# A layer norm's apply step divided between GpSimd and VectorE

## The reference, cut to what matters

```python
def _layernorm(x, axis=-1, eps=1e-05):
    m = jnp.mean(x, axis=axis, keepdims=True)
    v = jnp.var(x, axis=axis, keepdims=True)
    return (x - m) / jnp.sqrt(v + eps)
...
x = x + mixer(_layernorm(x))          # four times,
x = x + feed_forward(_layernorm(x))   # in turn
```

## Time and profile before

| | us |
|---|---|
| median of 3 runs | 810.92 (805.61 to 813.16) |
| the profiled execution: time | 812.87 |
| its span, first to last instruction | 811.2 |
| TensorE busy in the span | 668.7 (82%) |
| VectorE busy | 387.0 (48%) |
| ScalarE busy | 303.1 (37%) |
| GpSimd busy | 229.2 (28%) |

### The profile page before, as it was taken

The page is one execution under the profiler, slowest core; times in us unless marked ns, Lnnn a source line. Parts: engine busy times, 40 slices in busy tenths (PEclk is TensorE's granted clock), DMA queues, the critical chain, the costliest instruction groups (busy, mean ns, idle before and its releaser), DMA issues. The chain is left out here.

```text
span 811.2 us, 12856 instructions
## 1 busy us (share of the span) xinstructions
PE 668.7 (82%) x4034; PEld 556.4 (69%) x4034; DVE 387.0 (48%) x978; ACT 303.1 (37%) x604; POOL 229.2 (28%) x274
## 2 busy tenths in 40 slices
PE   4888936997996999957989983799995798898397
PEld 2476725685794899953677763699994367776296
DVE  4566816114445433314578756343440466885301
ACT  2344524232413344422434552235442243454222
POOL 5176620001200044442045400724334204541000
PEclk9989977798996899985899995899998589999599
DMA  3745720634206166533497503577653349840442
GB/s 90 195 114 142 176 57 0 156 99 96 48 1 175 40 161 160 121 48 65 131 248 212 111 17 113 149 177 183 170 124 48 70 132 233 222 114 1 102 119 72
DMA packets 92485, 95.14 MB, mean 117 GB/s; under 512 B 17313, under 2 KB 78644, under 8 KB 92424
## 3 DMA queue, kind: packets, MB, share of 16 engines
q1 hardware_dynamic: 78952, 74.91, 34.6%
q0 software_dynamic: 11808, 18.38, 11.3%
q10 hardware_dynamic: 1680, 1.28, 0.6%
HBM read 66.92 MB, written 27.84 MB: 117 GB/s over the span
## 5 line engine op out<-in xcount | busy, mean ns | idle before, releaser
L2017 POOL DMA_INDIRECT sum_scratch<-area,f_row_index x48 | 72.4, 1509 | 177.6 <-DVE area L1963 167.9
L881 DVE TENSOR_REDUCE neg_max<-psum 128x4 f32<-128x1024 f32 x72 | 87.9, 1221 | 31.0 <-PE psum L767 30.2
L1722 PE MATMUL psum<-w,area 128*112 128x192 f32 (+1 forms) x576 | 96.2, 326 | 0.0
L1722 PEld LDWEIGHTS psum<-w,area 128*112 128x112 f32 (+1 forms) x576 | 93.5, 183 | 0.0
L961 POOL TENSOR_TENSOR shift<-ident,neg_max 128x256 fp32r<-128x256 f32 x96 | 66.5, 704 | 84.8 <-DVE neg_max L881 56.4
L779 PE MATMUL psum<-q_parts,k_parts 128*128 128x256 f32 x288 | 78.5, 303 | 0.4
L780 PE MATMUL psum<-shift,ones_r 128*128 128x256 f32 x288 | 74.2, 289 | 0.0
L767 PE MATMUL psum<-k_parts,q_parts 128*128 128x256 f32 x288 | 52.9, 307 | 19.9 <-DVE neg_max L881 8.6
L1821 DVE TENSOR_TENSOR q_parts<-w,q_parts 128x1536 fp32r<-128x1536 f32 x16 | 28.1, 1758 | 82.7 <-ACT q_parts L1751 82.7
L779 PEld LDWEIGHTS psum<-q_parts,k_parts 128*128 128x128 f32 x288 | 56.7, 197 | 10.8 <-issue 8.2
L360 PE MATMUL psum<-ident,x_norm 128*96 128x128 f32 x128 | 26.1, 349 | 45.0 <-DVE x_norm L330 44.8
(11 more groups left out here) (250 smaller groups left out, 1328.9 us busy)
## 6 DMA issues: line engine op xcount, KB each, us to landing
w<-in_f_w_dram SPq DMA_DIRECT2D x32, 576.0 KB, 4.8
w<-in_f_w_dram SPq DMA_DIRECT2D x16, 384.0 KB, 4.4
w<-in_f_w_dram SPq DMA_DIRECT2D x32, 192.0 KB, 5.2
q_parts<-q_scratch SPq DMA_DIRECT2D x32, 192.0 KB, 3.6
q_scratch<-area SPq DMA_DIRECT2D x22, 192.0 KB, 2.1
k_parts<-k_scratch SPq DMA_DIRECT2D x63, 64.0 KB, 3.1
q_parts<-q_scratch SPq DMA_DIRECT2D x32, 96.0 KB, 2.9
q_parts<-q_scratch SPq DMA_DIRECT2D x40, 64.0 KB, 3.3
```

Source lines behind the costliest of these rows:

```text
L881: ins = dve.tensor_reduce(most, ps[:, 0:2, :].rearrange("p b (c k) -> p (b c) k", c=2), AX_X, ALU.max, negate=True)
L1722: ins = pe.matmul(ps[0:R, 6 + c // 2, D * (c % 2):D * (c % 2 + 1)], x.hidden[:, fc, R * c:R * (c + 1)], net.w2[:, b, fc, :], start=(fc == ...
L2017: pool.indirect_dma_start(net.sum_dram[:, :], bass.IndirectOffsetOnAxis(ap=row_index[0:size, b, c:c + 1], axis=0), x.y[0:size, b, c, :], N ...
```

## The change

Of each pair of tiles, VectorE normalises the even one and GpSimd the odd one. GpSimd waits for `rstd_ready`, the same signal that VectorE waits for, and signals a semaphore of its own, `normed_by_pool`. Whoever waited for `normed` now waits for both (`both`): TensorE before the transposes and before the forward transform, ScalarE and VectorE in the two steps of norm 5, and GpSimd before its bias add. GpSimd's four tiles of a norm stand where the diff puts them: alone in the blocks of norms 0, 1, 5 and 7; in the Fourier block those of norm 2 after the two DMAs, and those of norm 3 after the bias add; in the expert blocks after the last scatter-add.

```diff
--- before.py
+++ after.py
@@ -311,6 +311,7 @@
         self.aggregated = net.sem(tag + "_aggregated")
         self.rstd_ready = net.sem(tag + "_rstd_ready")
         self.normed = net.sem(tag + "_normed")
+        self.normed_by_pool = net.sem(tag + "_normed_by_pool")
         self.turned = net.sem(tag + "_turned")
 
     def stats(self, dve, q):
@@ -326,10 +327,21 @@
         dve.wait_ge(self.std_ready, q + 1)
         dve.reciprocal(net.rstd[:, 2 * q:2 * q + 2], net.std[:, 2 * q:2 * q + 2]).then_inc(self.rstd_ready, 1)
         dve.wait_ge(self.rstd_ready, q + 1)
-        for t in (2 * q, 2 * q + 1):
-            ins = dve.tensor_scalar(net.x_norm[:, t, 0:D], net.x_res[:, t, :], net.mean_var[:, t, 0:1],
-                                    net.rstd[:, t:t + 1], ALU.subtract, ALU.mult)
-        ins.then_inc(self.normed, 1)
+        self.tile(dve, 2 * q).then_inc(self.normed, 1)
+
+    def tile(self, eng, t):
+        net = self.net
+        return eng.tensor_scalar(net.x_norm[:, t, 0:D], net.x_res[:, t, :], net.mean_var[:, t, 0:1], net.rstd[:, t:t + 1],
+                                 ALU.subtract, ALU.mult)
+
+    def gpsimd(self, pool):
+        for q in range(PAIRS_OF_TILES):
+            pool.wait_ge(self.rstd_ready, q + 1)
+            self.tile(self.net.nc.gpsimd, 2 * q + 1).then_inc(self.normed_by_pool, 1)
+
+    def both(self, eng, q):
+        eng.wait_ge(self.normed, q + 1)
+        eng.wait_ge(self.normed_by_pool, q + 1)
 
     def vector(self, dve, loaded=None):
         for q in range(-1, PAIRS_OF_TILES):
@@ -344,7 +356,7 @@
     def tensor(self, pe):
         net = self.net
         for q in range(PAIRS_OF_TILES):
-            pe.wait_ge(self.normed, q + 1)
+            self.both(pe, q)
             if q == 3:
                 pe.wait_ge(self.x_chan_ready, 2)
             self.turn(pe, q, self.BANKS[q])
@@ -404,13 +416,13 @@
 
     def split_high(self, act, q):
         net, tiles = self.net, slice(2 * q, 2 * q + 2)
-        act.wait_ge(self.normed, q + 1)
+        self.both(act, q)
         act.copy(net.experts.high[:, tiles, :], net.x_norm[:, tiles, 0:D]).then_inc(self.tokens_high, 1)
 
     def split_low(self, dve, q):
         net, tiles = self.net, slice(2 * q, 2 * q + 2)
         dve.wait_ge(self.tokens_high, q + 1)
-        dve.wait_ge(self.normed, q + 1)
+        self.both(dve, q)
         dve.tensor_tensor(net.experts.low[:, tiles, :], net.x_norm[:, tiles, 0:D], net.experts.high[:, tiles, :], ALU.subtract)
 
 
@@ -432,6 +444,10 @@
         @block.scalar
         def _(act):
             norm.scalar(act)
+
+        @block.gpsimd
+        def _(pool):
+            norm.gpsimd(pool)
 
         @block.tensor
         def _(pe):
@@ -1133,7 +1153,7 @@
 
             for n in range(8):
                 i, half = n // 2, n % 2
-                pe.wait_ge(before.normed, i + 1)
+                before.both(pe, i)
                 for k in range(2):
                     ins = pe.matmul(ps[0:HC, n, 0:2 * BINS], net.x_norm[:, 2 * i + k, HC * half:HC * (half + 1)],
                                     f.fwd[:, k, :], start=(k == 0), stop=(k == 1))
@@ -1235,9 +1255,11 @@
             nc.gpsimd.dma_start(every, net.zeros[:, :, :].to_broadcast([P, E_MOE * SLOTS_MAX // P, ROW])).then_inc(slots_zeroed, DMA)
             nc.gpsimd.dma_start(net.sum_dram[TOK:, :].rearrange("(n p) f -> p n f", p=P),
                                 net.zeros[:, :, 0:D].to_broadcast([P, SLOTS_MAX // P, D])).then_inc(slots_zeroed, DMA)
-            pool.wait_ge(before.normed, PAIRS_OF_TILES)
+            before.gpsimd(pool)
+            before.both(pool, PAIRS_OF_TILES - 1)
             nc.gpsimd.tensor_tensor(net.x_res[:, :, :], net.x_res[:, :, :],
                                     f.bb[:, :, :].to_broadcast([P, TILES, D]), ALU.add).then_inc(bias_in, 1)
+            norm.gpsimd(pool)
             pool.wait_ge(slots_zeroed, 2 * DMA)
 
 
```

## The result

The changed kernel takes 819.23 us (median of 4 runs, 814.84 to 822.53), against 811.50 for four runs of the kernel before (805.61 to 813.16). The ratio is 1.0132 [1.0093, 1.0171]: 1.3% slower, where the prediction had 809.3 and a range up to 815.0. The profiled execution is 818.76 with a span of 816.9, against 812.87 and 811.2.

What follows compares the result with a forecast made beforehand. VectorE was taken to set the pace of most pairs in the norms. Gains of 0.5, 1.1 and 0.5 less losses of 0.38 and 0.06 gave -1.7 us, so 809.3 us from the median 810.92, range 805 to 815.

Steps and rivals of the forecast that it cites:

- Part 2: GpSimd's apply step in every norm: 0.45 us per 128x192 tile, bounds 0.34 and 0.61, from GpSimd's copy and two-input rows.
- X: Time of one 128x192 apply step on GpSimd, taken as 0.45 us, between 0.34 and 0.61.
- the 0.13 read from VectorE: Cost of reading two values per partition, from VectorE's 378 less 249 ns, added to 0.48 for the upper bound 0.61.
- the prediction's own slope of 1.3 us per 0.1: Over all eight norms, each 0.1 us more of GpSimd's step costs about 1.3 us, starting from a sum of -1.7.
- the method of following the pairs: Each norm's pairs of tiles followed as a relay from reciprocal through apply steps to TensorE's transposes; sum -1.7 us.
- the rival given 0.17: GpSimd is slow at the apply step: X from 0.61 to 1.2; more than 1% slower (+8.1) at 1.2; chance 0.17.
- Part 3: VectorE's and GpSimd's apply steps exclude each other; VectorE goes first for 0.29 us, and GpSimd's X starts after that.
- The relay: Per pair, from the reciprocal's start to TensorE's transposes: 0.96 us with the change against 0.90 before.
- The row of 3.45 us: Fourier stage: VectorE's 96x144 step shown for 3.45 us beside GpSimd's bias add, read as the engines excluding each other.
- the predicted stretch of the last pair in norms 1 and 7: VectorE's apply step of the last pair there stretched by 0.2, as GpSimd's previous tile holds it up.
- Part 1: In the norms, one apply step leaves VectorE: 0.29 us less per pair, counting where VectorE bounds the pair's successor.
- Part 4: The sum norm by norm: norms 0, 4, 6 -0.5; 1, 7 -1.1; 5 -0.5; 2 +0.38; 3 +0.06; total -1.7 us.

Runs made afterwards that it cites:

- the small kernel: Not the network: single GpSimd instructions, each released by a VectorE reciprocal, alone and beside a VectorE instruction, 16 settings; GpSimd's 128x192 apply step took 1.00 us alone.
- 2, 3 and 5 shared: The change in norms 2, 3 and 5 only, VectorE keeping all tiles elsewhere, against the kernel before: 815.20 against 808.51, ratio 1.0076.
- 4 and 6 shared: The change in norms 4 and 6 only, VectorE keeping all tiles elsewhere, against the kernel before: 813.76 against 808.51, ratio 1.0032.

## Why the prediction was wrong

**Part 2, the price of the step: the term that failed.** The prediction took X = 0.45 with 0.34 and 0.61 as bounds. It is 1.00 alone. The steps of the bound were reasonable one by one and wrong in kind: a one-input operation need not cost less than a two-input one on GpSimd (0.70 with a single operation against 0.59, itself above the 0.476 worked out), and the second operation and the values together cost 0.30 there, not the 0.13 read from VectorE. Nor are the 0.13 shown to be the price of the values: in the small kernel VectorE's own apply step, values and all, takes 0.25 when it follows another VectorE instruction without a wait, and 0.38 when it is released. The bound was built from another engine's rows and from the cheapest operations of this one. With X = 1.00 the prediction's own slope of 1.3 us per 0.1 gives -1.7 + 7.2 = +5.5. Norm by norm that is +0.93 for norms 0, 4 and 6 (measured +0.79, and +0.83 and +0.80 with the drain out of the way), 0.55 for norms 1 and 7 (+0.20, +0.11), 0.61 for norm 3 (+0.77), 0.93 for norm 2 (at least 1.15), 0.05 for norm 5 (+1.94, mostly the clock's). So the method of following the pairs held in the main; its most uncertain term was far off, and it fell in the rival given 0.17, whose price for it would have been 816.4 from the median (810.92 + 5.5). The remaining 2.8 us to the measured 819.23 are not this term's.

The Trainium skill, in "GPSIMD Engine Reference", section 4.1, calls GpSimd about twice as slow for two-input operations and "roughly line-rate" for one-input ones. The runs here do not agree for this one-input form: 1.00 us against VectorE's 0.38, and in the slope 3.3 ns a column against 0.52 ((1.08 - 0.38) / 1344, by the steps of 1536 and 192 columns).

**Part 3, the exclusion: right in its sum by luck, wrong in its parts.** The relay was worked out as 0.96 with X = 0.45, that is 1.51 with X = 1.00. Measured in norm 0: 1.48 to 1.53. But behind a reciprocal of 0.13 it is made of 0.10 to GpSimd's start after the reciprocal, 1.00, 0.11 of exclusion and 0.15 to TensorE, not of 0.25 of waiting, 1.00 and 0.05. The row of 3.45 us was read rightly as an exclusion, and extended too far: it came from a two-input operation of 1536 columns, which held VectorE up. GpSimd's apply step never held up VectorE's, in no norm (378 to 381 ns) and in no setting of the small kernel, so the predicted stretch of the last pair in norms 1 and 7 didn't come, and these two norms lost less than the sum has for X = 1.00. The Trainium skill says, in "SBUF — State Buffer", section "Who interferes with whom", that whoever issues first blocks the other fully, for the whole instruction. Here GpSimd's step started up to 0.3 us ahead of VectorE's and didn't block it; the one that stood back was GpSimd, for 0.33 us then and for 0.10 when VectorE's came first. Its copy, on the other hand, cost VectorE 0.10, and the apply step cost VectorE's small steps in the Fourier stage 0.15.

**Part 1, VectorE's saving:** right. The second reciprocal came 0.30 earlier in norm 0, and the copy in place of the step showed the saving pass on to the norm.

**Part 4, norm 2:** the mechanism (the DMA issue holds up GpSimd's first tile) was right. The loss was 1.15 by the same sum with X = 1.00 and the longer DMA issue and handovers, not 0.38. "The 32 matmuls then run 9.62 us as one piece, so nothing gives this back" missed that it could grow: with the start 1.15 late they took 11.5 (197.44 to 208.94). Of the 1.9 more, one late pair is 0.38 and the longer time at the lower clock some 1.3. That the late start causes the longer time is not shown: 2, 3 and 5 shared gave a start as late with a short time at the lower level (3.0 us, +1.59), 4 and 6 shared a start on time with a longer one (4.4 us, +0.56).

**Missed altogether: the drain.** The prediction put at nothing whatever the added work pushes behind it on GpSimd in norms 4 and 6, since the scatter-adds are over when they begin. They are, but the drain that ends GpSimd's part of the block was hidden beside the norm, and now it comes after it: 2.2 us, shown by moving it back.

**The rest.** The sum of stages is 10.7. The prediction's formulas with X = 1.00 give 5.5 of it, about 1 too much for norms 0, 1, 3, 4, 6 and 7 together; the drain is 2.2, norm 2 beyond X 2.1, and norm 5 beyond X 1.9. In these last two most is time at the lower clock, which varies by more than a microsecond from one trace to the next. Whether the change has a share in it is open.

## What to carry to other kernels

Before work is given to an engine that is idle, price that very instruction on that very engine: form, number of operations and kinds of operands; a bound from its cheaper operations is no bound. An engine that is added to a short relay must be as fast as the one it relieves, handovers included; here it had 0.77 us to beat from the reciprocal's end to the transposes (0.04 + 0.67 + 0.06) and took 1.36 (0.10 + 1.11 + 0.15); with a third of the tile it was still 0.93. And look at what the added work pushes behind it at the next meeting of all engines: a drain that was hidden comes out. When stages are compared between single traces, look where in each the granted clock fell or rose before a difference is given to the change.

## What the runs showed of the hardware

- GpSimd's apply step (one input, two operations, two values per partition, f32) of 128x192: 1.00 us; with two numbers 0.86, with one value and one operation 0.76, with one number 0.70; the two-input add 0.59, the copy 0.34.
- Released together with VectorE's instructions on the same kind of data it grew by 0.10 (192 columns), 0.81 (1536 columns) and 1.57 (two-input add of 1536 columns), beside one that reads PSUM by nothing, and it stretched none of them. It stretched VectorE's steps of 96x144 in the Fourier stage from 0.22 to 0.36 and 0.37. GpSimd's copy stretched VectorE's apply step from 0.38 to 0.48.
- A drain of GpSimd behind indirect scatter-adds takes 2.0 and 3.3 us in the two blocks, whether it comes at once or behind four more instructions, 14 us later (377.39 to 379.4, and 640.27 to 643.6). Behind the norm's tiles alone, in norm 0, it ends 0.06 after the last of them.
- From the start of VectorE's reciprocal of 0.17 us to GpSimd's next start: 0.27. From GpSimd's end to TensorE's start: 0.14 to 0.15.
- Eight small matmuls of the expert logits take 0.96 us at the higher granted clock and 1.71 at the lower; four of the forward transform 0.97 and 1.92.
